# Product-key layer: the first block's products and selection in the similarities' stage, the last five pairs behind the last similarities

## What is computed

```python
q = batch_norm(x @ w_q)                       # 16 query parts (8 heads x 2 sides) of 128
sims = q_part . keys[part]                    # 64 keys in each part
vx, ix = top_k(sims of side 0, 8)             # 8 best keys of either side
vy, iy = top_k(sims of side 1, 8)
all_scores = vx[..., :, None] + vy[..., None, :]
scores, pos = top_k(all_scores, 8)            # 8 best of the 64 pairs, in each head
experts = ix[pos // 8] * 64 + iy[pos % 8]
hidden = gelu(x . down_embed[experts]) * softmax(scores)
out = hidden @ up_embed[experts]              # summed over heads and choices
```

## Time and profile before

| | us |
|---|---|
| median of 3 runs | 2365.23 (2355.63 to 2367.0) |
| the profiled execution | 2356.12 |
| its span in the profile | 2354.3 |
| TensorE busy | 2101.9 (89%) |
| VectorE busy | 1593.6 (68%) |
| ScalarE busy | 1002.9 (43%) |
| GpSimd busy | 886.1 (38%) |
| mean granted clock of TensorE | 0.958 of 2.4 GHz |

### The profile page before, as it was taken

The page is one execution under the profiler, slowest core; times in us unless marked ns, Lnnn a source line. Parts: engine busy times, 40 slices in busy tenths (PEclk is TensorE's granted clock), DMA queues, the critical chain, the costliest instruction groups (busy, mean ns, idle before and its releaser), DMA issues. The chain is left out here.

```text
span 2354.3 us, 33922 instructions
## 1 busy us (share of the span) xinstructions
PE 2101.9 (89%) x12230; PEld 1455.0 (62%) x12230; DVE 1593.6 (68%) x4159; ACT 1002.9 (43%) x2133; POOL 886.1 (38%) x545
## 2 busy tenths in 40 slices
PE   8688888899996899698996888999898899999996
PEld 3255555554663799466483444448556788888886
DVE  6799999833657112556128996706687988888886
ACT  2498988623866231365425775241102221222110
POOL 0298888401642895333103665414211111110110
PEclk9799999999998999899997999999999999999998
DMA  3131111000005567300101000020300000000001
GB/s 103 47 94 50 50 50 47 17 12 1 1 1 194 188 227 231 117 2 2 61 1 43 1 1 23 21 81 1 143 1 3 1 1 1 1 1 1 1 1 37
DMA packets 63514, 109.35 MB, mean 46 GB/s; under 512 B 12530, under 2 KB 44146, under 8 KB 61620
## 3 DMA queue, kind: packets, MB, share of 16 engines
q1 hardware_dynamic: 61812, 102.99, 13.4%
q0 software_dynamic: 1536, 4.20, 0.5%
HBM read 94.19 MB, written 12.98 MB: 46 GB/s over the span
## 5 line engine op out<-in xcount | busy, mean ns | idle before, releaser
L781 POOL TENSOR_TENSOR XT<-mamba_DU,scan_BS 128x1024 f32<-128x1024 f32 x128 | 299.2, 2361 | 141.9 <-DMA scan_BS<-mamba_rows 104.2
L910 DVE TENSOR_TENSOR_SCAN scan_H<-scan_AB,XT 128x512 f32<-128x512 f32 x256 | 296.4, 1209 | 7.9 <-POOL XT L781 4.9
L3291 PE MATMUL ex_HP<-XT,pe_DOWN 128*128 128x256 f32 x1024 | 250.1, 391 | 6.0 <-PEq L3027 5.2
L3352 ACT ACTIVATE ex_GH<-ex_HP 128x512 f32<-128x512 f32 x128 | 76.5, 599 | 380.8 <-PE ex_HP L3291 346.1
L3322 PE MATMUL ex_OP<-pe_UP,ex_GH 128*128 128x256 f32 x1024 | 231.5, 380 | 0.0
L795 PEld LDWEIGHTS scan_TP<-ident,scan_H 128*128 128x128 f32 x1024 | 120.6, 142 | 156.8 <-DVE scan_H L910 79.8
L840 ACT ACTIVATE scan_AB<-mamba_E,mamba_AA 128x510 f32<-128x510 f32 x256 | 198.7, 776 | 37.2 <-DVE scan_H L910 32.9
L3291 PEld LDWEIGHTS ex_HP<-XT,pe_DOWN 128*128 128x128 f32 x1024 | 194.3, 194 | 31.8 <-issue 5.4
L3322 PEld LDWEIGHTS ex_OP<-pe_UP,ex_GH 128*128 128x128 f32 x1024 | 194.1, 190 | 26.2
L804 PE MATMUL scan_YT<-mamba_BC,ident 128*128 128x512 f32 x384 | 199.0, 601 | 4.1 <-ACT scan_YS L856 2.3
L3378 POOL TENSOR_TENSOR ex_AS<-ex_AS,pe_IV 128x512 f16<-128x512 f16 x32 | 52.9, 1682 | 363.4 <-DVE ex_AS L3426 363.4
(11 more groups left out here) (452 smaller groups left out, 4390.2 us busy)
## 6 DMA issues: line engine op xcount, KB each, us to landing
moe_W<-in_L_ffn_w SPq DMA_DIRECT2D x32, 1024.0 KB, 7.6
scan_BS<-mamba_rows SPq DMA_DIRECT2D x64, 256.0 KB, 3.2
pe_DOWN<-in_L_ffn_down SPq DMA_DIRECT2D x1, 4096.0 KB, 12.9
pe_UP<-in_L_ffn_up SPq DMA_DIRECT2D x1, 4096.0 KB, 22.3
moe_dispatch<-moe_BOTH SPq DMA_DIRECT2D x1, 2560.0 KB, 13.8
experts_XE<-moe_dispatch SPq DMA_DIRECT2D x16, 160.0 KB, 2.4
moe_answers<-experts_YE SPq DMA_DIRECT2D x16, 160.0 KB, 3.6
XT<-in_xT SPq DMA_DIRECT2D x4, 512.0 KB, 5.8
```

The costliest lines, as they stand in the source:

```text
L781: pool.tensor_tensor(BU[:, r % 2, cs], tokens(DU, cs, r // DS), row, ALU.mult).then_inc(bu_ready, 1)
L910: v.tensor_tensor_scan(H[:, r % 2, c], AB[:, n % 2, :], BU[:, r % 2, c], 0.0, ALU.mult, ALU.add).then_inc(h_ready, 1)
L3291: ins = pe.matmul(HP[:, n % 2, a, :], DOWN[:, k, 2 * q + a, :], XT[:, k, b * BLK:(b + 1) * BLK], start=(k == 0), stop=(k == KD - 1))
```

## The change

- The selection becomes a class, `Selection`, whose buffers live in `stage_peer`. Its instructions are those of before.
- The first block's sums, hits, Exp and five steps move into the last group of the similarities' stage: sums behind GpSimd's unit 0, the steps behind VectorE's scans of units 2 to 6, the hits behind GpSimd's unit 3, the Exp at ScalarE's unit 4.
- The first block's 16 pairs of products move there too: one behind unit 7 of group 0, five each in groups 1 and 2 (behind units 0, 1, 2, 6, 7), five behind the last similarities, then the transposes of the keys. They use one PSUM bank, `HP`, for which the products of the fold and their transposes now share one bank; the fold waits for the copy of the group before's transposes.
- Small buffers of the stage move into buffers of `Selection` and of `GH`; the key numbers and ranks are loaded between DOWN and UP.
- The experts' stage starts with a pair of block 1 and the first unit's gates; its selection steps are those of blocks 1 to 7.

```diff
@@ peer_sides, buffers
-        WTP = st.ps("WTP", [P, CG // 2, D])
-        TP = st.ps("TP", [P, KD, CK])
+        FT = st.ps("FT", [P, 512])
+        WTP = FT[:].rearrange("p (j d) -> p j d", j=CG // 2)
+        TP = FT[:].rearrange("p (k c) -> p k c", k=KD)
+        HP = st.ps("HP", [P, 2, BLK])
...
+        HIDDEN_AT = [(0, 7)] + [(g, u) for g in (1, 2) for u in (0, 1, 2, 6, 7)]
+        SELECT_AT = 2
@@ sync
-                expert_loads.issue(sp)
+                down_loads.issue(sp)
+                up_loads.issue(sp)
@@ tensor
+                def hid(q):
+                    if q == 0:
+                        down_loads.wait(pe)
+                    else:
+                        pe.wait_ge(hidden_read, q)
+                    for a in range(2):
+                        for k in range(KD):
+                            ins = pe.matmul(HP[:, a, :], DOWN[:, k, 2 * q + a, :], XT[:, k, 0:BLK], start=(k == 0), stop=(k == KD - 1))
+                    ins.then_inc(hidden, 1)
+
+                def turn_keys():
+                    pe.wait_ge(chosen.arranged, 1)
+                    for part, qs in ((0, (0, 1)), (1, (2,))):
+                        pe.wait_ge(hidden_read, J2 // 2 + part)
+                        for q in qs:
+                            for a in range(chosen.TB):
+                                ins = pe.transpose(HP[:, q % 2, a * P:(a + 1) * P], chosen.DUP[:, q, a].rearrange("p a k -> p (a k)"), ident[:, 0:P])
+                        ins.then_inc(hidden, 1)
...
                     if g:
-                        pe.wait_ge(folded_copied, g)
+                        pe.wait_ge(turned_copied, g)
...
+                        if (g, u) in HIDDEN_AT:
+                            hid(HIDDEN_AT.index((g, u)))
+                for q in range(len(HIDDEN_AT), J2 // 2):
+                    hid(q)
+                turn_keys()
@@ scalar
                 for g in range(NGR):
-                    std(g)
-                    copies(g)
+                    for u in range(UN):
+                        if g + 1 < NGR and u == SCALE_AT:
+                            std(g + 1)
+                        if g + 1 < NGR and u == TURN_AT:
+                            copies(g + 1)
+                        if (g, u) in HIDDEN_AT:
+                            hidden_out(HIDDEN_AT.index((g, u)))
+                        if g == NGR - 1 and u == SELECT_AT + chosen.TB:
+                            chosen.exponentials(act, 0)
+                for q in range(len(HIDDEN_AT), J2 // 2):
+                    hidden_out(q)
@@ vector
+                        elif u >= SELECT_AT:
+                            if u == SELECT_AT:
+                                up_loads.wait(v)
+                            chosen.step(v, ch, u - SELECT_AT, 0)
@@ gpsimd
+                        if g == NGR - 1 and u == 0:
+                            chosen.sums(pool, 0, 0)
+                        if g == NGR - 1 and u == SELECT_AT + chosen.TB - 1:
+                            chosen.hits(pool, 0, 0)
@@ peer_experts, tensor
-                expert_loads.wait(pe)
-                for u in range(UB):
-                    for q in range(PU):
-                        hid(0, u * PU + q)
-                    if u == TURN_AT:
-                        turn(0)
                 for n in range(NU):
                     b, u = n // UB, n % UB
+                    if n == 0:
+                        hid(b + 1, 0)
                     gates(n)
@@ peer_experts, vector
-                v.wait_ge(loaded, 32)
-                for u in range(UB):
-                    select_step(0, u)
                 sides(0)
```

More of the change, by code:

```diff
@@ L2963, in _, with peer_sides @@
                     act.activation(GS[:, m, 0:D + 1], GP[:, m, 0:D + 1], ACT.Copy, scale=1.0 / T)
-def peer_sides(nc, XT, ident, SV, IV, expert_loads, inputs):
+def peer_sides(nc, XT, ident, SV, IV, DOWN, GH, chosen, down_loads, up_loads, inputs):
     CG = 4
@@ L3113, in copies, with hidden_out @@
                     act.activation(WP[:, :, g * CK:(g + 1) * CK], TP[:], ACT.Copy).then_inc(turned_copied, 1)
-                for g in range(NGR):
-                    std(g)
-                    copies(g)
+                def hidden_out(q):
+                    act.wait_ge(hidden, q + 1)
+                    act.activation(GH[:, 2 * q:2 * q + 2, :], HP[:], ACT.Gelu_apprx_tanh).then_inc(hidden_read, 1)
+                std(0)
+                copies(0)
+                for g in range(NGR):
+                    for u in range(UN):
[9 more added lines that the diff above has]
+                    hidden_out(q)
+                for part in range(2):
+                    act.wait_ge(hidden, J2 // 2 + part + 1)
+                    if part == 0:
+                        act.activation(chosen.KEYS[:, 0, 0:2, :], HP[:], ACT.Copy).then_inc(hidden_read, 1)
+                    else:
+                        act.activation(chosen.KEYS[:, 0, 2, :], HP[:, 0, :], ACT.Copy).then_inc(hidden_read, 1)
             @block.vector
@@ L3258, in peer_experts @@
         OP = st.ps("OP", [P, 2, 512])
-        loaded = st.sem("loaded")
         hidden = st.sem("hidden")
@@ L3345, in _ @@
             def _(act):
-                for b in range(NB):
+                for b in range(1, NB):
                     for q in range(NP):
@@ L3364, in _ @@
             def _(pool):
-                for b in range(NB):
-                    if b:
-                        pool.wait_ge(hits_read, b)
-                    for a in range(TB):
-                        t = b * TB + a
-                        sx = SV[:, t, 0:PH, :].rearrange("p h (a o) -> p h a o", o=1).to_broadcast([P, PH, PK, PK])
-                        sy = SV[:, t, PH:, :].rearrange("p h (o b) -> p h o b", o=1).to_broadcast([P, PH, PK, PK])
-                        pool.tensor_tensor(AS[:, a], sx, sy, ALU.add).then_inc(summed, 1)
-                    pool.wait_ge(ranks_ready, b + 1)
-                    for side in range(2):
-                        for a in range(TB):
-                            hit = HIT[:, side, a].rearrange("p (h k) r -> p h k r", h=PH)
-                            key = IV[:, b * TB + a, side * PH:(side + 1) * PH, :].rearrange("p h (o r) -> p h o r", o=1).to_broadcast([P, PH, PK, PK])
-                            ins = pool.tensor_tensor(hit, hit, key, ALU.mult)
-                    ins.then_inc(hits_ready, 1)
+                for b in range(1, NB):
+                    chosen.sums(pool, b, b - 1)
+                    chosen.hits(pool, b, b - 1)
             @block.vector
@@ L3396, in numbers @@
                         return IOTA[:, 0:n].rearrange("p (o n) t -> p o n t", o=1).to_broadcast([P, UNIT // RUN, n, RUN])
-                    if n % UB == 0:
+                    if b and n % UB == 0:
                         v.wait_ge(hidden_read, turn_place(b, 1) + 1)
@@ L3420, in ranks @@
-                def ranks():
-                    ch.link(v.tensor_scalar(AB[:, 0], AB[:, 1], 3, None, ALU.logical_shift_right))
-                    ch.link(v.tensor_scalar(AB[:, 1], AB[:, 1], PK - 1, None, ALU.bitwise_and))
-                    ch.link(v.tensor_copy(RF[:], AB[:]))
-                    for side in range(2):
-                        rank = RF[:, side].rearrange("p (n o) -> p n o", o=1).to_broadcast([P, TB * HK, PK])
-                        ins = v.tensor_tensor(HIT[:, side].rearrange("p a n r -> p (a n) r"), rank,
-                                              RANKS[:].rearrange("p (o r) -> p o r", o=1).to_broadcast([P, TB * HK, PK]), ALU.is_equal)
-                    ins.then_inc(ranks_ready, 1)
@@ L3430, in keys @@
-                def keys(b):
-                    v.wait_ge(hits_ready, b + 1)
-                    for side in range(2):
-                        for a in range(TB):
-                            ins = v.tensor_reduce(DUP[:, side, a, 0, :], HIT[:, side, a], AX_X, ALU.add)
-                    ins.then_inc(hits_read, 1)
-                    v.wait_ge(hits_read, b + 1)
-                    left, right, upper = DUP[:, 0, :, 0, :], DUP[:, 1, :, 0, :], DUP[:, 1, :, 1, :]
-                    ch.link(v.tensor_scalar(upper, right, float(J2), float(NK), ALU.is_ge, ALU.mult))
-                    v.tensor_tensor(left, left, upper, ALU.add)
-                    ch.link(v.scalar_tensor_tensor(right, upper, -float(J2) / NK, right, ALU.mult, ALU.add))
-                    for side in range(2):
-                        v.tensor_copy(DUP[:, side, :, 1, :], DUP[:, side, :, 0, :])
@@ L3455, in select_step @@
-                def select_step(b, u):
-                    if u < TB:
-                        pick(b, u)
-                    elif u == TB:
-                        ranks()
-                    elif u == 3:
-                        keys(b)
-                    elif u == 4:
-                        probabilities(b)
-                v.wait_ge(loaded, 32)
-                for u in range(UB):
-                    select_step(0, u)
                 sides(0)
```

198 lines of the change are left out of this document (131 added, 67 removed).

## The result

| | before | after |
|---|---|---|
| median (18 runs each) | 2365.20 us | 2380.76 us |
| fastest and slowest run | 2355.04, 2391.32 | 2366.21, 2403.28 |
| the profiled execution, its span | 2356.12, 2354.3 | 2369.52, 2367.7 |
| ratio after / before | | 1.0064, 95% 1.0036 to 1.0093 |
| TensorE, VectorE busy | 2101.9, 1593.6 | 2109.6, 1594.9 |

The changed kernel is slower by 0.64%, some 15 us, and 13.4 us in the profiled executions. The prediction said +7.5 us (2372.7, range 2358 to 2384): the median lies inside the range, but it moved by twice the forecast.

The account below looks back on a forecast made before the run. TensorE was taken to bound the first three groups of the similarities' stage, VectorE the last. 18.0 + 15.9 - 26.5 - 0.65 + 0.8 = +7.5 us on the median 2365.2 gave 2372.7 us, range 2358 to 2384.

Parts of the forecast that it names:

- The bound: TensorE bounds similarities' groups 0 to 2, VectorE the last group; TensorE has no slack behind 1867 to absorb a delay.
- (a): Groups 0 to 2: eleven moved pairs paid in full on TensorE at 1.77 us each, less filled 0.50 us gaps: +18.0 us.
- groups 1 and 2 some 36.8 us long each: Sign in the similarities' stage that the forecast holds, with VectorE idle before its scans; 28.4 us would mean pairs cost nothing.
- slow clock: Rival: TensorE at 1.2 GHz in groups 1 and 2 and the pairs behind the last similarities; up to +18.6, 2383.8 us; 23%.
- (b): Last group: block 0's selection paid in full on VectorE, including a 1.4 us wait for hits: +15.9 us (bounds 15.9 and 18.8).
- slow hits: Rival in the last group: GpSimd's hits take 6.98 us beside the scans, +2.9 us, 2375.6 us; 15%.
- (c): Opening of the experts' stage: 27.2 us before VectorE's first comparison removed, 0.65 of stage change stays: -26.5 us.
- (f): Five pairs and keys' transposes behind the last similarities: covered by VectorE's work, 0; late copies up to +1.3 us or more.
- (d): Before the first gated products: four pairs ahead of the gates gone, and VectorE's wait for the gates with them: -0.65 us.
- (e): Start of the experts' stage: GpSimd's sums for block 1 slow the first comparisons beside them: +0.8 us (0 to 1.6).
- (g): Similarities' stage: ScalarE's four or five more table changes of 1.28 us each hide behind a scan: 0.
- free ride: Rival: TensorE really waits for VectorE in groups 0 to 2, so the eleven pairs cost nothing: -10.5, 2354.7 us; 12%.

Follow-up runs that it names:

- after_again: The changed kernel run once more, no edit: median 2391.72 us, 1.0101 of before; 161.89 us from first similarities to first gated product (157.11 in its first profile).
- after_third: The changed kernel run again, no edit, beside the kernel before and two others: median 2382.72 us, 1.0078 of before; 161.89 us from first similarities to first gated product.
- best2: Changed kernel with pairs ahead of folds, five in the last group, two in the experts' stage, GpSimd's sums beside the last scan: 2349.08 us, 0.9936 of before.
- group3: Changed kernel with five pairs in the last group, three behind the last similarities, eight in groups 0 to 2: 152.39 us to first gated product, for 157.11.
- sums: Changed kernel with GpSimd's sums for block 1 at the end of the similarities' stage: 156.34 us from first similarities to first gated product, for 157.11.
- pairs_only: Changed kernel with only the pairs moved, the selection left opening the experts' stage: 170.38 us from first similarities to first gated product, for 146.69 before.
- tail16: Changed kernel with all 16 pairs of block 0 behind the last similarities: 171.88 us from first similarities to first gated product, for 157.11.
- gap: Changed kernel with one pair of each of groups 0 to 2 ahead of the fold: 149.39 us from first similarities to first gated product, for 157.11.
- gap_timed: The kernel with a pair ahead of each fold, in more runs: median 2368.07 us, 1.0014 of before; 151.73 us from first similarities to first gated product.
- best: Changed kernel with pairs ahead of folds, five in the last group, two in the experts' stage, GpSimd's sums behind its last cast: 2350.94 us, 0.9985 of before.

## Why the prediction was right or wrong, point by point

**The bound.** Right. In groups 0 to 2 TensorE was the only bound, as VectorE's waits for it show; in the last group VectorE was, with 35.9 of 38.1 us; and nothing behind took up the delay.

**(a) Eleven pairs, +18.0.** Measured +1.26, +9.62 and +8.10, 19.0 in all. Group 2 gives the pair's term clean: 8.10 for 8.35. The step that was mis-sized is the clock: the fall in group 1, 1.6 us before, is 3.1 after. The sum had carried over the 1.6 of before (29.95 + 8.35 = 38.3 for group 1), while the sign "groups 1 and 2 some 36.8 us long each" had left it out. I had the clock as a rival, with 3.2 us over the two groups; `after_again` and `after_third` are that rival, with 1.6 us in groups 1 and 2 and 3.1 in group 0.

**(b) The selection, +15.9.** Measured 38.10 - 22.32 = 15.8. The hits took 4.10 beside scans, the wait for them 1.43 (forecast 1.4), L2879 and L2880 0.29 and 0.28 us as taken from their shortest. The rival of slow hits fell in every run, `best2` among them (4.09). The Trainium skill (GPSIMD Engine Reference, Key points) has GpSimd contend with VectorE's instructions that have two SBUF inputs or run in a two-port mode. The trace agrees from both sides: hits of 4.10 beside scans, and comparisons of 1.60 and 3.04 us beside the sums, for 0.69 and 2.29.

**(c) Removed, -26.5, and (f) the tail, 0.** The opening is gone, but 1.85 us of stage change stand where I left 0.65: +1.2. It is (f) that failed, at its upper end (I wrote up to +1.3). I had the pairs' end at 15.1 us behind the fifth scan and the last scan to cover transposes and copies. TensorE's similarities behind the fifth scan started at 1815.00 and the pairs ended at 1831.80, 16.8 behind: the last similarities ran at the low clock (2.08 us for 1.13 at 1816.87) and took 4.1 us, where I had 2.5 with TensorE at full clock. From the pairs' end to the end of the last copy it is 2.95 us (1831.80 to 1834.75); from 15.1 us behind the fifth scan this would just have been covered. `after_again` and `after_third` show the clock's share: with the same tail and the last similarities slower still (2.08 us from the start), the change of stage is 1.6 longer. In `group3` and `best2`, with three pairs in the tail and full clock in the last similarities, it is 0.66.

**(d) The gates, -0.65.** Right: no wait before 1844.02.

**(e) The sums beside the comparisons, +0.8.** Measured 1.66: 0.91 on R, 0.75 on L. I had transferred the loss of one line (0.75) once; both comparisons lie in GpSimd's stretch of 2.54 us, and I gave 1.6 only as the upper bound. `sums` shows the cause.

**(g) Table changes, 0.** Right: seven table loads of 1.28 us stand between 1713.07 and 1812.52, for three in the opening before, and group 2 with two of them still came in at 8.10 for 8.35.

**What the sum left out.** 0.9 us behind the first gated product: 0.57 in the last change of stage, 0.3 over the 64 units. No experiment was made on either, so their cause is open. From the first gated product to the end it is 522.8 us in both profiles of before and 523.6 to 523.7 in all profiles of changed versions but three: 523.3 in `pairs_only`, 525.4 in `after_again` and `after_third`. The rows of VectorE at the end, before and after:

```profile
2338.20 1.41 DVE L454 BATCH_NORM_STATS2 last_raw<-X 128x6 f32<-128x256 f32 x4 [1.41 <-PEq L3523]
```

```profile
2351.58 1.41 DVE L454 BATCH_NORM_STATS2 last_raw<-X 128x6 f32<-128x256 f32 x4 [1.98 <-PEq L3601]
```

So 7.5 became 10.4, up to rounding, by +1.0 (a: +1.5 for the clock, -0.5 for the pairs), -0.1 (b), +1.2 (f), +0.9 (e); with 0.9 behind it is 11.3, close to the difference of the fastest runs (2366.21 - 2355.04 = 11.2). The sign, the two halves and the reason (each half lands on the engine that is full there) held.

**The rivals.** The free ride is shown wrong by `tail16` and `pairs_only`. The slow hits never came. The slow clock came in part: 1.5 us more in group 1 and 1.2 in the change of stage in the first profile of after, 4.8 more in the two others, never the 11.1 of the rival, since the tail pairs behind the first ran at 1.99 or 2.00 us in each.

**The median.** It moved by 15.6 us, more than 11.3, and the sum has no term for it. That it stayed in the range rests on the range's width and not on the sum. Two of the three profiled executions of after lost 6.5 us more than the one behind the 11.3 (4.8 in the local measure, 1.7 behind it). If they are the usual case, the difference is 11.3 to 17.8 us, an estimate from these three profiles in which 15.6 lies. The routing stage, in the last section, adds to it by an amount that no run here settles.

## What to carry to other kernels

Before moving work beside other work, look at which engine is full in each stretch: here TensorE's pairs went to where TensorE was full and VectorE's selection to where VectorE was full, though TensorE had 8 us free in the last group (five pairs there cost nothing) and 1.95 in every fold. Put moved work into the idle rows that the timeline shows one by one, not beside the engine with the lower busy share. A helper moved off the path, such as GpSimd's sums, counts twice: with what runs beside it, and with the barrier that waits for it.

## What the runs showed of the hardware that was not expected

**A pair in the fold's gap kept the clock up.** Behind TensorE's wait of 1.95 us the clock fell to 0.50 in 17 of 30 groups, over the ten profiles that have the gap, and cost 1.4 to 3.1 us each time. In the four with a pair in the gap (`gap`, `gap_timed`, `best`, `best2`) it fell in none of 12. The same 1.95 us gap gives both outcomes. In three executions (`after_again`, `after_third`, `group3`) the clock was at 0.50 already behind the fold ahead of group 0, and there all nine groups had the fall; in the seven others it was 8 of 21. What decides it in one execution is open.

**A busy TensorE can stay at 1.2 GHz.** In 4 of 14 profiled executions (`tail16`, `group3`, `after_again`, `best2`) the clock stayed at 0.50 through the routing stage of the sublayer of experts, where no version differs, though TensorE was busy throughout. The same two lines of TensorE in `after` and in `after_again`, and a stretch of each:

```profile
740.59 9.91 PE L1200 MATMUL route_ring<-moe_TT,route_WK 128*128 128x512 f32 x16
750.43 20.15 PE L1205 MATMUL route_ring<-route_WV,moe_TT 128*128 128x256 f32 x64
```

```profile
756.00:760.00 4.00, 4.00 (x14) 1.93 (x14) 3.79 (x9) 4.00 (x10) 3.08 (x4) 1.00 0.28 98
```

```profile
741.03 15.94 PE L1200 MATMUL route_ring<-moe_TT,route_WK 128*128 128x512 f32 x16
756.90 36.87 PE L1205 MATMUL route_ring<-route_WV,moe_TT 128*128 128x256 f32 x64
```

```profile
756.00:760.00 4.00, 4.00 (x8) 1.50 (x6) 1.95 (x5) 4.00 (x9) 3.07 (x4) 0.50 0.28 98
```

Both come out of a wait of 10.28 us for VectorE at 0.50; in `after` the clock rose early in L1200, in `after_again` it had not after 50 us without idle. That costs 22 to 23 us. The Trainium skill (TensorE: Matmul & The Clock Gate, What's actually happening) has activity release the throttle. In the other ten executions the trace agrees; in these four no release came in the 50 us, and the measurement decides.

One thing ahead of the stretch sorts the 14 executions. In the four, sixteen matmuls of the router (L1449) took 3.64 us and the four transposes behind them (L1453) 0.66, full clock. In the ten others it rose either within L1449 (3.36 to 3.57 us) or not before the transposes (1.12 us). Rows of `after`, `after_again` and `after_third`:

```profile
723.37 3.53 PE L1449 MATMUL route_LT<-XT,route_GW 128*32 128x512 f32 x16 [5.15 <-DMA route_TI<-in_spill_rows]
727.79 0.66 PE L1453 MATMUL route_LP<-ident,route_LS 128*128 128x128 f32 x4 [0.90 <-DVE route_LS L1476]
```

```profile
723.70 3.64 PE L1449 MATMUL route_LT<-XT,route_GW 128*32 128x512 f32 x16 [5.14 <-DMA route_TI<-in_spill_rows]
728.23 0.66 PE L1453 MATMUL route_LP<-ident,route_LS 128*128 128x128 f32 x4 [0.89 <-DVE route_LS L1476]
```

```profile
726.93 3.64 PE L1449 MATMUL route_LT<-XT,route_GW 128*32 128x512 f32 x16 [6.23 <-DMA route_TI<-in_spill_rows]
731.46 1.12 PE L1453 MATMUL route_LP<-ident,route_LS 128*128 128x128 f32 x4 [0.89 <-DVE route_LS L1476]
```

So the moment of an earlier rise goes with the outcome 15 us later. This was read off afterwards and nothing was changed to test it; the start of the stretch itself (738.4 to 744.7 us) doesn't sort them.

It bears on the medians. Runs more than 15 us above the fastest of their kernel were 19 of 36 for after, 19 of 93 for before, 3 of 12 for `gap_timed` and 4 of 24 for `best` and `best2`. The mark of 15 us is no clean sign of the routing stage: the profiled execution of `after_third`, at 2382.77 us and 16.6 above the fastest, had full clock there and lost its time elsewhere. More than 20 us above were 16 of 36 for after and 17 of 93 for before, which pure chance would seldom give. But nearly half of the excess lies in one set of six runs (4 of 6 beside 1 of 17); in the two larger sets it was 7 of 18 beside 4 of 18, and 5 of 12 beside 9 of 29. For `after_third`, which asked this, its rival's half came (7 of 12 above 15 us) and its one in ten didn't (9 of 29, 3 of 12 and 2 of 12 for the others). Whether the version changes the odds of a stage 900 us earlier therefore stays open, as do the steps of 2 to 8 us in the start of the similarities' stage between profiles of unchanged code.
